# A GNN layer kernel: the instructions of VectorE, ScalarE and TensorE in another order within a step, and a last edge chunk on 128 partitions

## The reference, cut to what matters

```python
# x: 50000 x 128, edges: 25000 (src, dst), dst sorted, edge_attr: 25000 x 128; all float32
x0 = relu(layernorm(x))                      # no gamma, no beta
xn = layernorm(x0, g1, b1)
msg = relu(xn[src] + edge_attr)
aggr = segment_sum(msg, dst)                 # 50000 rows
h = (1 + eps_gin) * xn + aggr
h = relu(h @ Wg1 + bg1) @ Wg2 + bg2
x2 = x0 + h
xn2 = layernorm(x2, g2, b2)
f = gelu(xn2 @ Wf1 + bf1) @ Wf2 + bf2        # 128 -> 512 -> 128
return x + x2 + f
```

## Time and profile before

| | us |
|---|---|
| median of 3 runs (1043.13 to 1047.68) | 1045.61 |
| the profiled execution | 1042.96 |
| its span, from first to last instruction | 1041.2 |

### The profile page before, as it was taken

How to read it: one execution, slowest core, us unless ns; L and a number is a source line. 1 busy time by engine, 2 the same in 40 slices (tenths; PEclk the granted TensorE clock), 3 DMA queues, 4 the chain that set the end, 5 groups by cost and what they waited for, 6 DMA issues and landing times. The chain is left out here.

```text
span 1041.2 us, 23085 instructions
## 1 busy us (share of the span) xinstructions
PE 982.8 (94%) x6684; PEld 857.0 (82%) x6684; DVE 965.1 (93%) x3499; ACT 852.8 (82%) x2158; POOL 825.9 (79%) x510
## 2 busy tenths in 40 slices
PE   1569999999999999999999999999999999999978
PEld 0357888988889889889888889889889889888867
DVE  5979999999999999999999999999999999998642
ACT  1458888898888988988888988988988988978853
POOL 7788888888788888888888888888888888876610
PEclk9869999999999999999999999999999999999999
DMA  7856766877886654555654664654654554543221
GB/s 259 228 165 162 204 172 179 242 230 220 253 238 157 160 130 118 157 133 117 156 135 116 154 139 116 157 136 115 158 134 116 150 140 117 125 105 81 51 60 41
DMA packets 110468, 156.87 MB, mean 151 GB/s; under 512 B 24835, under 2 KB 50607, under 8 KB 110334
## 3 DMA queue, kind: packets, MB, share of 16 engines
q1 hardware_dynamic: 70358, 128.99, 39.0%
q0 software_dynamic: 37760, 25.66, 17.7%
q10 hardware_dynamic: 2216, 0.66, 0.3%
HBM read 90.61 MB, written 64.61 MB: 149 GB/s over the span
## 5 line engine op out<-in xcount | busy, mean ns | idle before, releaser
L451 POOL DMA_INDIRECT aggr_sums<-e_merged,e_index x196 | 339.2, 1731 | 80.6 <-issue 70.7
L939 PE MATMUL p_out<-wf,n_act 128*128 128x128 f32 x3136 | 370.5, 276 | 1.6
L939 PEld LDWEIGHTS p_out<-wf,n_act 128*128 128x128 f32 x3136 | 357.7, 191 | 6.9 <-DVE p_out L855 5.9
L460 POOL TENSOR_TENSOR n_rstd<-n_var,minus_half 128x16 f32<-128x16 f32 (+3 forms) x102 | 259.7, 2557 | 48.3 <-DVE n_var L835 32.2
L532 ACT ACTIVATE n_act<-p_f,bf1e_col 128x512 f32<-128x512 f32 x392 | 256.2, 680 | 35.2 <-PE p_f L902 31.3
L440 POOL DMA_INDIRECT e_x<-in_x,e_cols x196 | 223.2, 1139 | 61.0 <-issue 59.4
L902 PE MATMUL p_f<-n_z2T_high,wf_low 128*128 128x512 f32 x392 | 202.0, 515 | 5.6 <-DVE n_z2T_low L701 4.8
L902 PE MATMUL p_f<-n_z2T_high,wf_high 128*128 128x512 f32 x392 | 155.1, 396 | 0.0
L902 PE MATMUL p_f<-n_z2T_low,wf_high 128*128 128x512 f32 x392 | 154.6, 394 | 0.0
L687 DVE BATCH_NORM_STATS2 n_stat<-n_x 128x6 f32<-128x256 f32 x392 | 140.3, 418 | 0.6 <-issue 0.4
L614 ACT ACTIVATE n_inT<-p_in 128x512 f32<-128x512 f32 x98 | 58.5, 597 | 99.0 <-PE p_in L946 99.0
(11 more groups left out here) (85 smaller groups left out, 1455.4 us busy)
## 6 DMA issues: line engine op xcount, KB each, us to landing
n_x<-in_x SPq DMA_DIRECT2D x97, 256.0 KB, 3.0
n_aggr<-aggr_sums SPq DMA_DIRECT2D x97, 256.0 KB, 2.7
out_dram<-n_out SPq DMA_DIRECT2D x97, 256.0 KB
aggr_sums<-zeros SPq DMA_DIRECT2D x26, 512.0 KB, 5.2
e_dst<-in_dst_rows SPq DMA_DIRECT2D x49, 256.0 KB, 3.8
e_attr<-in_attr SPq DMA_DIRECT2D x48, 256.0 KB, 3.5
aggr_sums<-zeros SPq DMA_DIRECT2D x12, 1024.0 KB, 5.7
e_x<-in_x,e_cols POOLq DMA_INDIRECT x196, 3.7
```

What stands on the lines that cost most here:

```text
L451: nc.gpsimd.indirect_dma_start(out=aggr, out_offset=bass.IndirectOffsetOnAxis(ap=e_index[0:r, s, j:j + 1], axis=0), in_=e_merged[0:r, s, j ...
L460: return nc.gpsimd.tensor_tensor(n_rstd[0:r, s, lo:hi], n_var[0:r, s, lo:hi], minus_half[0:r, 0:(hi - lo) * J].rearrange("p (a j) -> p a j ...
L939: last = nc.tensor.matmul(p_out[0:b.rows, j, :], n_act[:, k, j, 0:b.rows], wf2[:, k, :], start=False, stop=(k == KF - 1), skip_group_check ...
```

## The change

The four compute engines' `step` functions are written anew, with separate orders for odd and even steps.

- **VectorE**: what was in `first_half`, `second_half` and inline in `step` is cut into small functions with the same instructions. The statistics of relu and their variance are of node(1) (they were of node(0)), `n_zg` is of node(2) (it was of node(1)), and x2 is taken last in a step, of node(3), in place of first, of node(4).
- **TensorE**: the transposes of `n_in` are of node(3) at the start of an odd step and second in an even one (they were of node(2) at the end). The fourth quarter of the second product is issued in the next step, of node(7). `p_g` and `p_gout` sit between quarters.
- **ScalarE**: gelu of quarter 0 is of node(5) at the end of a step, and so are `n_inT` and the first two `seed_gout`, of node(2). `merged_rows` takes over the waits for the zeroed parts and for the chunk before.
- **GpSimd**: the first pair of scatters comes behind the gathers in even steps, and waits for `s_emerged` alone. FIRST_JOINED is LEAD - 1 = 2. Gathers and scatters are always on 128 partitions; for rows past r, `e_index` is filled with spare rows behind the sums (L846).
- SyncE's instructions are the same and in the same order. The number of matmuls, activations and DVE instructions on tensors is the same, but for the L846 of chunk 48.

```diff
-        FIRST_JOINED = 4
+        FIRST_JOINED = LEAD - 1
...
             def gather(c, columns):
...
-                        out=e_x[0:r, s, j, :], out_offset=None, in_=x,
-                        in_offset=bass.IndirectOffsetOnAxis(ap=e_cols[0:r, s, 0, j:j + 1], axis=0),
+                        out=e_x[0:P, s, j, :], out_offset=None, in_=x,
+                        in_offset=bass.IndirectOffsetOnAxis(ap=e_cols[0:P, s, 0, j:j + 1], axis=0),
...
             def scatter_pair(c, g):
...
-                            ap=e_index[0:r, s, j:j + 1], axis=0),
-                        in_=e_merged[0:r, s, j, :], in_offset=None,
+                            ap=e_index[0:P, s, j:j + 1], axis=0),
+                        in_=e_merged[0:P, s, j, :], in_offset=None,
...
                     pool.wait_ge(s_emerged, c.at + 1)
-                    pool.wait_ge(s_eindex, c.at + 1)
+                    if apart:
+                        pool.wait_ge(s_eindex, c.at + 1)
...
-                    if not apart:
-                        for q in s_zeroed[zeroed_for(c.k - 1) if c.k else 0:zeroed_for(c.k)]:
-                            pool.wait_ge(q, 32)
-
-                    if not c.is_number(0):
+                    if apart and not c.is_number(0):
                         pool.wait_ge(q_scatter[(c.k - 1) % 3], SCATTERED * (c.value + (c.k - 1) // 3 + 1))
...
                 if 1 in halves and not 0 in halves:
+                    if (c := edge(0)) is not None:
+                        gather(c, range(PAIR, J))
                     merged_first(edge, apart)
...
-            def merged_rows(c):
+            def merged_rows(c, apart):
...
+                    if not apart:
+                        for q in s_zeroed[zeroed_for(c.k - 1) if c.k else 0:zeroed_for(c.k)]:
+                            act.wait_ge(q, 32)
+                        if not c.is_number(0):
+                            act.wait_ge(q_scatter[(c.k - 1) % 3], SCATTERED * ((c.k - 1) // 3 + 1))
...
+            def edge_index(c):
...
+                    if r < P:
+                        lo = r // 32 * 32
+                        nc.vector.tensor_copy(e_index[lo:P, s], spare[lo:P]).then_inc(s_spare_rows, 1)
+                        dve.wait_ge(s_spare_rows, 1)
...
                 if 0 in halves or not halves:
-                    first_half(edge(1), node)
...
+                    scale_by_gamma(node(2))
+                    variance0_of(node(1))
+                    relu_stats(node(1))
+                    take_out(node(7))
+                    x2_stats(node(4))
+                    variance_of(node(1))
+                    add_sums(node(2))
+                    add_x(node(6))
+                    x2_variance(node(4))
+                    edge_x_stats(edge(1))
+                    x_stats(node(0))
+                    edge_x_small(edge(1))
+                    x_minus(node(0))
+                    z2_low(node(5))
+                    add_b1(None if alone(node, apart) else edge(2))
+                    edge_match(edge(1))
+                    take_x2(node(3))
                 if 1 in halves:
-                    second_half(edge(1), None if alone(node, apart) else edge(2), node, apart)
...
+                    x_stats(node(0))
+                    x2_stats(node(4))
+                    scale_by_gamma(node(2))
+                    variance0_of(node(1))
+                    relu_stats(node(1))
+                    edge_relu_stats(edge(1))
+                    x2_variance(node(4))
+                    variance_of(node(1))
+                    take_out(node(7))
+                    sum_of(None if alone(node, apart) else edge(2), apart)
+                    edge_variance(edge(1), apart)
+                    x_minus(node(0))
+                    add_x(node(6))
+                    z2_low(node(5))
+                    edge_scaling(edge(1))
+                    edge_index(edge(1))
+                    add_sums(node(2))
+                    take_x2(node(3))
```

More of the change, by code:

```diff
@@ L516, in step @@
                     merged_first(edge, apart)
-                if 1 in halves and (c := edge(0)) is not None:
+                if 1 in halves and 0 in halves and (c := edge(0)) is not None:
                     gather(c, range(PAIR, J))
@@ L575, in step @@
-                if 1 in halves and 0 not in halves and (c := edge(3)) is not None and not c.is_number(0):
-                    merged_rows(c)
-                if (b := node(0)) is not None:
-                    r = b.rows
-                    act.wait_ge(s_nminus, b.at + 1)
-                    reached(act, s_nzg, b.at - 3)
-                    for j in range(J):
-                        last = nc.scalar.activation(n_relu[0:r, b.slot(4), j, :], n_x[0:r, b.slot(8), j, :], ACT.Relu,
-                                                    bias=n_minus[0:r, b.slot(8), j:j + 1])
-                    last.then_inc(s_nrelu, 1)
@@ new lines, in add_sums @@
+            def add_sums(b):
+                if b is not None:
+                    r, s = b.rows, b.slot(8)
+                    dve.wait_ge(s_nzg, b.at + 1)
+                    dve.wait_ge(s_nrstd, b.at + 1)
+                    dve.wait_ge(q_aggr[b.slot(4)], 16 * (b.uses(4) + 1))
+                    reached(dve, s_tin, b.at - 1)
+                    for j in range(J):
+                        last = nc.vector.scalar_tensor_tensor(n_in[0:r, b.slot(2), j, :], n_zg[0:r, b.slot(2), j, :],
+                                                              n_rstd[0:r, s, 1, j:j + 1], n_aggr[0:r, b.slot(4), j, :],
+                                                              ALU.mult, ALU.add)
+                    last.then_inc(s_nin, 1)
```

547 lines of the change are left out of this document (334 added, 213 removed).

## The result

The changed kernel takes 1041.78 us (median of 12 runs, 1040.30 to 1045.22), the kernel before beside it 1046.32 us (12 runs). The ratio is 0.996, 95% interval 0.9946 to 0.9975. The forecast was 1027.3 us, so about 14 us of the expected 18 are missing. The prediction took 0.5% (5.2 us) for no change; the 4.5 us lie within that, though the interval leaves out 1.

A forecast was written before the change was run, and what follows sets the result against it. DVE was taken as the bound, 19.40 us per pair of steps. Tail -9.0, steady part -7.0 and head -2.3 sum to -18.3 us: 1042.96 to 1024.7, put at 1027.3 because the runs' median lies 2.65 higher; range 1018.5 to 1038.

The forecast's parts named there:

- The tail, -9.0: After x2 of block 86: last chunk on 128 partitions shortens scatters and the wait for sums; -9.0 us, bounds -5 and -11.
- The head, -2.3: At the start: chunks 2 and 3 lose a power of 1.62 us each; -2.3 us, bounds 0 and -5.
- n_in's wait for n_aggr: Steady part: 7.1 us of DVE waits in 15 places; later n_in gives slack, within a steady-part term of -7.0 us.
- the slack of 0.9 us in the even step: Even step: n_aggr is there at 17.4 us and n_in stands at 18.3, where before there was no slack.
- POOL: Steady part: a pair needs 18.7 us of POOL; rival that stretched gathers and scatters make it the bound, 1065 us, chance 0.09.
- The failed step: Steady part: gelu of quarter 0 a step earlier removes a wait of PE and none of DVE; costed at nothing.
- the two chains that were worked out: Steady part: scatters to n_aggr to n_in, and POOL's power to n_z and n_relu to relu statistics; slack 0.9 us each.
- What would show it: Profile signs: pairs at 19.40 to 19.50 us, n_aggr waits below 3 us, last scatters at 1.65 us, no 10 us wait.
- The waits only move: Steady part: one 0.9 us slack is missing, DVE stalls about 0.2 us a pair as before; 1034 us, chance 0.22.

The follow-up runs named there:

- the last chunk alone: The kernel before with only the last chunk's gathers and scatters on 128 partitions and the spare indices filled: 1035.35 us, ratio 0.9875.
- n_out late: The changed kernel with n_out of the odd step moved behind the statistics of x2 and n_var of the relu, about 1.0 us later: 1032.19 us, ratio 0.9859.
- even p_out<-n_x early: The changed kernel with p_out<-n_x of the even step 1.2 us earlier in VectorE's order, ahead of the four e_sum: 1029.95 us, ratio 0.9828.
- the dose at n_out: The changed kernel with n_out of the odd step 0.67 us earlier in VectorE's order, ahead of the relu statistics: 1064.21 us, ratio 1.0171.
- the first theory's other end: The changed kernel with p_out<-n_x of the odd step moved straight behind n_out, to release TensorE 2.4 us earlier: 1059.56 us, ratio 1.0132.

## Why the prediction was wrong, and where it was right

- **The tail, -9.0:** right in the windows. -7.7 in the changed kernel, -8.7 from the last chunk alone, +8.6 when it is undone. That 106 partitions were the cause is shown by these two runs. In medians it is 12.1 and 6.8 us. The Trainium skill (DMA: Bandwidth & Descriptors, Why a DMA increments its semaphore by 16 and not by 1) had it so; the trace agrees in the times, 1.59 and 1.55 us for a scatter that took 2.79, though no row here counts the engines that served one.
- **The head, -2.3:** -1.5, about as much as this stretch differs between kernels with the same orders.
- **n_in's wait for n_aggr:** half right. From 340 us on it went (2.6 us to none), as the slack of 0.9 us in the even step said. But the odd step's n_in, 4.0 us behind x2 (603.95 to 607.97 where it does not wait), waits 3.5 us between 200 and 340 us. No chain was worked out for it.
- **POOL:** not the bound, as said: with POOL's order as changed, pairs come down to 19.44 once n_out's wait is gone. Gathers took 1.12 us in the mean, scatters 1.65.
- **The failed step** is the one on the carried-over part of FFN2: "gelu of quarter 0 a step earlier removes a wait of PE and none of DVE, so it is costed at nothing; its cover is DVE", and before it "no row in which DVE waits for them here". The carried fourth quarter is not named there; it was taken for PE's work only, and the term was put at nothing. But n_out waits for it, and the change put n_out early in the odd step, behind n_zg and the relu's statistics. Had the chain been worked out, it would have been: from the end of p_out<-n_x, four quarters at 3.57/4 = 0.89 us and p_in between them 0.47 (604.10 to 604.57 in the rows above), 4.2 us with hand-overs, beside 5.1 us of DVE's (601.26 to 606.34). Slack 0.9, like the two chains that were worked out: a third place to doubt, but no price. It wasn't enough, since the semaphore came 0.95 us later than the records of PE, and no row of the kernel before shows that. The runs put the loss at 10.0 us by the windows (832.7 for 822.7 with n_out late), 9.6 by the medians, of the 14.7 us by which the steady part missed.
- **What would show it:** the pair's 19.71 us lay outside the 19.40 to 19.50 that was asked for, but none of the three signs of being wrong came up (gathers over 1.3 us, DVE waiting for n_relu, ACT waiting for scatters ahead of e_merged). They watched the chains that had been worked out, and not this one.
- **"The waits only move"** (0.22) is what happened by its name and its 0.2 us a pair, but not by its mechanism: neither of the two chains that it names gave the stall. By its price it would have been 1034 us. It came dearer: n_out's 8.1 us and n_in's 3.5 together are more than the 7.1 of before, and 32 of the 42 pairs have their share.
- With that one wait away the changed kernel takes 1029.6 to 1032.2 us (five runs), 2 to 5 us over the forecast. As ratios they are 0.9823 to 0.9859, where the forecast's was 1027.3 / 1045.61 = 0.9825; but they come there in part by luck, with a last chunk that gave more by the medians than its -9.0 and a steady part that gains, by the windows, 2 to 4.5 us and not 7. Over 19.40 us a pair, its first 13 pairs, to about 340 us, still hold 4.6 us (even p_out<-n_x early) or 5.6 (n_out late), where the kernel before holds 4.8; the other 29 pairs hold 2.3, where it holds 5.4. The last part of the sums is zeroed at 325 us; that this is the cause was not tested.
- Two readings of the prediction are off by little: by its rows the gather that began during e_sum ended 0.98 us after it (504.69 to 503.71), not 1.06, and by its own formula the kernel would be slower than before from 1.24 us of stretch on, not 1.15. Neither moves the forecast.

The best kernels here are the changed one with the even p_out<-n_x 1.1 or 1.2 us earlier (ratios 0.9826 and 0.9828), and the latter with n_out late as well (0.9823), which no run tells apart. All beat both kernels, by a few moved lines of VectorE's order.

## What to carry to other kernels

When work is carried over into the next step, work out the chain of whoever reads its result, not only of the engine that does it: from the release, through everything queued ahead, to the reader's place in its own order. A slack of 0.9 us in a chain through TensorE was none here. Price the parts of a change apart, too: here one of them alone beat the whole. And move the waiting instruction or its releaser by a known amount in both directions before believing in a ring: the dose at n_out was right to 0.1 us, while the first theory's other end was not.
